# Cross-attention and a ternary feed-forward on one core: another lead-in, and the exponential taken while the transposed banks are read

## The chip, the cores and the metric

One NeuronCore of a Trainium2 chip. TensorE, VectorE, ScalarE, GpSimd and SyncE each run one instruction stream in order; they meet through semaphores. The metric is the device time of one execution in microseconds. Three runs of the kernel before took 98.30, 98.36 and 98.38 us, median 98.36.

## The reference, cut to what matters

```python
x = x + xattn(layernorm(x), ctx_512, Wq, Wkv_expand, Wout)
x = x + ffn(layernorm(x), w_gate, w_up, w_down)

def xattn(q, latent_kv, Wq, Wkv_expand, Wout):   # q (16, 56, 256), latent_kv (16, 1500, 64)
    kv = latent_kv @ Wkv_expand.T                # Wkv_expand (512, 64): 256 rows for k, 256 for v
    # 16 heads of 16; causal mask from query 0 and key 0
    attn = softmax(where(causal, qh @ kh.T / 4, min))
    return (attn @ vh) @ Wout.T

def ffn(x, w_gate, w_up, w_down):                # 256 -> 1024 -> 256
    # each weight: scale = mean(|w|), values -1, 0, 1; each token: scale = max(|x|) / 127, rounded
    return qlinear(silu(qlinear(x, w_gate)) * qlinear(x, w_up), w_down)
```

There are 56 queries, so the causal mask leaves the first 56 of the 1500 keys of each batch; only these are loaded.

## The kernel before, in words

The 16 batches of 56 tokens are 896 tokens, 7 tiles of 128. Attention goes by 8 pairs of batches (u = 0 to 7). All of it is float32 but the ternary feed-forward products. The order of the work is written out by hand: a lead-in, called slot -1, then slots 0 to 17. Each engine runs through the same slots and takes from each the work that tables at the top of the file give it (lines 22 to 68). In slot s TensorE does the scores of pair s, the transposes of the attention of pair s - 2, the transposes of the probabilities of pair s - 1, the jobs that `MISC_JOBS` lists for the slot (line 41), an output projection where `OP_SLOTS` has one, and the products of pair s - 1 with v (lines 1130 to 1149). From slot 8 on it does gate and up products, transposes of the rounded hidden values, and the down products.

Every small product goes into one of four PSUM banks, taken in turn: job number n writes bank n mod 4 when the job n - 4 has been read (`take_bank`, line 904). `VECTOR_READS` (line 49) says which of these banks VectorE reads; ScalarE reads the others (`read_misc`, line 336).

**The lead-in.** SyncE issues the loads x0, ctx0, ctx1, x1, x2 and the weights of the feed-forward; ScalarE's queue issues wkv, wq, ctx2, ctx3 (lines 34 and 35). The four ctx loads move rows of 256 bytes (one key of one batch) to 56 partitions each, the wkv load rows of 256 bytes too. When wkv has landed, ScalarE writes it out twice side by side (line 323), so that four 128x128 transposes (line 939) give `wkvT` with the same 64 rows on both halves of the partitions. TensorE meanwhile runs nine products of zeros (`warm_up`, line 1076), then the jobs wkvT, three more products of zeros, ctxT (line 945: waits for all four ctx loads), two more, wqT, the first quarter of k of batches 0 to 7, xT of tile 0, and q of pair 0. The first two tiles' layer norm is done by VectorE with GpSimd's reciprocal root (lines 471 and 683), tiles 2 to 6 by GpSimd (`first_layer_norm`, line 463: two small operations, a power, one normalising operation).

**k.** `kT` holds k transposed; `k_wide` holds it once for each of four heads with the other heads' rows zeroed (`widen`, line 286), so that one product gives the scores of four heads. The first part is widened by VectorE and GpSimd in the lead-in, the rest by GpSimd in slots 0 to 3. Index c of `kT` is the half of the batches (0 to 7, 8 to 15); c = 1 is computed in slot 2.

**Softmax.** VectorE takes the maxima out of PSUM (line 715) and writes the differences into `probs` (line 724). ScalarE exponentiates them in place (line 567). TensorE transposes them, eight 128x128 transposes into two banks (line 1031). ScalarE copies the banks into `pT` (job kind "tr", line 367). TensorE multiplies with v; VectorE divides by the sums (line 730).

**The slots around it.** `ABS_SLOTS` puts the sum of magnitudes of the three weights to slot 1 (VectorE), 2 and 3 (ScalarE); a product with a constant matrix (job kind "mean") gives the scale, ScalarE reads it, and VectorE inverts it in the same slot (`invert_weight_scale`, line 798), ahead of the next slot's division of the attention. ScalarE loads the tables for silu behind its other work of slot 7 (line 570).

Of the kernel before, what the change touches and what calls it, by code (L numbers as in the profile page):

```python
# [24 lines left out]
LN1_SLOTS = {-1: [2], 0: [3], 1: [4], 2: [5], 3: [6]}  # L25
# [26 lines left out]

EXP_BEHIND = {0: 3}
# [17 lines left out]
def xattn_ffn(nc, x, ctx_512, wq, wkv, wout, w_gate, w_up, w_down, out):  # L71
# [38 lines left out]
    DV = 2  # L110
# [30 lines left out]
    with ExitStack() as ctx:  # L141
# [28 lines left out]
        probs = sb("probs", [P, R, NH, Q])  # L170
# [48 lines left out]
        ctx2_in = sem("ctx2_in")  # L219
        wkv_in, wq_in, wo_in, wkv_ready = sem("wkv_in"), sem("wq_in"), sem("wo_in"), sem("wkv_ready")  # L220
# [20 lines left out]
        exp_ready, rden_ready = sem("exp_ready"), sem("rden_ready")  # L241
# [44 lines left out]
        def widen(eng, ops, slot, engine):  # L286
            for c, hf, g in WIDENINGS.get((slot, engine), []):
                j0, j1 = KEY_GROUPS[c][g]
                cols = slice(2 * S * j0, 2 * S * j1)
                n = 2 * S * (j1 - j0)  # L290
                const(eng, "head_mask")
                wait_read(eng, *[job for job in K_JOBS if job[1] == c and job[2][0] <= j0 < job[2][1] and hf in job[3]])
                ops.tensor_tensor(k_wide[:, c, hf, :, cols], kT[:, c, hf, None, cols].to_broadcast([P, RH, n]),  # L293
                                  head_mask[:, 0:RH, None].to_broadcast([P, RH, n]),
                                  ALU.mult).then_inc(kw_ready[c][g], 1)
# [15 lines left out]
        def load(eng, name):  # L311
# [91 lines left out]
        def _(pool):  # L403
# [141 lines left out]
        def _(act):  # L545
# [17 lines left out]
            def exponentials(s):  # L563
                u = s
                if 0 <= u < NP:
                    act.wait_ge(sub_ready, u + 1)
                    nc.scalar.activation(probs[:, u % R, :, 0:S], probs[:, u % R, :, 0:S],  # L567
                                         ACT.Exp).then_inc(exp_ready, 1)

            def load_silu_tables(s):  # L570
                if s == NP - 1:
                    load_tables(ACT.Silu)
# [55 lines left out]
            for s in range(NT_SLOT0):  # L628
                read_attention(s - 2)
                read_probabilities(s)  # L630
                read_misc_banks(s, 0, EXP_BEHIND.get(s, 0))
                exponentials(s)
                read_misc_banks(s, EXP_BEHIND.get(s, 0), None)
                ternary_signs(s)
                sum_magnitudes(s)
                load_silu_tables(s)
            for s in range(NT_SLOT0, SLOTS):
                if s == NT_SLOT0:
                    read_attention(s - 2)
                read_probabilities(s)  # L640
# [9 lines left out]
        def _(dve):  # L650
# [18 lines left out]
            nc.vector.memset(probs[:, :, :, S:], 0.0).then_inc(pads_ready, 1)  # L669
# [25 lines left out]
            widen(dve, nc.vector, -1, "vector")  # L695
# [22 lines left out]
            def subtract_maxima(s):  # L718
                u = s
                if u < NP:  # L720
# [3 lines left out]
                    nc.vector.tensor_tensor(probs[:, u % R, :, 0:S].rearrange("p (r h) k -> p r h k", r=2),  # L724
# [134 lines left out]
            for s in range(NT_SLOT0):  # L859
# [15 lines left out]
                widen_k(s)  # L875
# [24 lines left out]
        def _(pe):  # L900
# [9 lines left out]
            def write_values(i):  # L910
# [3 lines left out]
                wait_read(pe, ("wkvT", 0), ("ctxT", 0))  # L914
# [13 lines left out]
            def write_misc(job):  # L928
# [245 lines left out]
```

## Time and profile before

| | us |
|---|---|
| median of 3 runs (98.30 to 98.38) | 98.36 |
| span of the profiled execution | 99.1 |
| TensorE busy (share of the span) | 81.9 (83%) |
| VectorE busy | 72.4 (73%) |
| ScalarE busy | 58.6 (59%) |
| GpSimd busy | 56.9 (57%) |

The profile is of one execution, whose span is 99.1 us; its starts are counted from the first instruction. In the rows PE is TensorE, PEld its weight loads, DVE VectorE, ACT ScalarE, POOL GpSimd. A float32 product shows as two passes ("x8" for four products), a transpose as one. Many products are recorded by one helper (line 902), so they are told apart by their tiles: `sc` is the scores' PSUM, `bank` one of the four banks, `sc<-tern` the products of zeros. The starts of the first score products of a slot (`sc<-causal,sel`) mark the slots.

### The profile page before, as it was taken

What the parts mean: (1) busy time and instruction counts of PE and PEld (TensorE: products, weight loads), DVE (VectorE), ACT (ScalarE), POOL (GpSimd) and SP (SyncE); (2) the same over time, 40 slices, a digit from 0 to 9 for tenths busy, and PEclk for the clock granted to TensorE, in tenths of its full rate; (3) what the DMA queues carried; (4) which work ended last, traced back from release to release, by engine and by line L of the source; (5) the groups of instructions that cost most, each with busy time, mean ns of one, the idle gap of its engine ahead of it and who ended that gap; (6) DMA issues with size and microseconds to landing.
All of it is one profiled execution on the core that took longest, in us unless ns stands there. A gap on an engine that the chain in (4) does not pass through costs nothing.

```text
span 99.1 us, 2411 instructions
## 1 busy us (share of the span) xinstructions
PE 81.9 (83%) x872; PEld 57.4 (58%) x872; DVE 72.4 (73%) x180; ACT 58.6 (59%) x98; POOL 56.9 (57%) x109
## 2 busy tenths in 40 slices
PE   4964968976989985999999998699938589998680
PEld 1323645744865874878696876585514256665460
DVE  4650243978995898189976999637899999999741
ACT  0730241363528794657979699964565496988520
POOL 5640064739930989879693982526165651786650
PEclk9997599999999999999999999999999999999999
DMA  2999998000000000000089451800000000011123
GB/s 35 286 285 353 350 362 320 13 0 0 0 0 7 0 3 3 7 0 0 0 60 161 99 119 25 187 0 0 0 7 0 0 0 0 3 53 53 60 82 130
DMA packets 12579, 7.59 MB, mean 77 GB/s; under 512 B 7960, under 2 KB 12312, under 8 KB 12568
## 3 DMA queue, kind: packets, MB, share of 16 engines
q1 hardware_dynamic: 11292, 6.93, 26.1%
q10 hardware_dynamic: 1276, 0.51, 2.0%
q8 instruction: 7, 0.11, 0.5%
q14 instruction: 4, 0.03, 0.1%
HBM read 4.95 MB, written 0.92 MB: 59 GB/s over the span
## 4 chain that ended last, share of the span: by engine, by line
DVE 41%; PE 37%; issue 7%; DMA 6%; POOL 2%; ACTq 2%; ACT 1%; POOLq 0%; DVEq 0%
PE bank L902 21%; DVE amax L820 9%; DVE h_sb L813 7%; PE sc L902 7%; DMA ctx_sb<-in_ctx_dram 6%; DVE probs L724 4%; PE bank L1031 4%; DVE v_wide L655 3%; PE bank L1055 2%; DVE asum L708 2%; DVE mx L715 2%; DVE xnT L656 2%; DVE attn L739 2%; DVE s_tok L827 1%; DVE x_sb L755 1%
## 5 line engine op out<-in xcount | busy, mean ns | idle before, releaser
L293 POOL TENSOR_TENSOR k_wide<-kT,head_mask 128x896 f32<-128x896 f32 (+1 forms) x9 | 13.2, 1481 | 12.0 <-ACT kT L557 12.0
L902 PE MATMUL sc<-wT,xqT 128*128 128x512 bf16 x56 | 13.9, 380 | 3.4 <-DVE h_sb L813 3.4
L306 POOL TENSOR_SCALAR wf_sb<-h_sb,r_tok 128x512 f32<-128x512 f32 x13 | 9.1, 714 | 10.5 <-DVE r_tok L834 10.5
L612 ACT ACTIVATE wf_sb<-sc,s_out 128x512 f32<-128x512 f32 x14 | 9.6, 689 | 7.5 <-PE sc L902 5.1
L715 DVE TENSOR_REDUCE mx<-sc 128x16 f32<-128x896 f32 x8 | 8.7, 1090 | 3.6 <-PE sc L902 3.4
L813 DVE SCALAR_TENSOR_TENSOR h_sb<-sc,s_out,wf_sb 128x512 f32<-128x512 f32 x14 | 9.9, 740 | 1.1 <-ACT wf_sb L612 1.1
L902 PEld LDWEIGHTS sc<-wT,xqT 128*128 128x128 bf16 x56 | 5.0, 98 | 9.2 <-DVE h_sb L813 5.1
L567 ACT ACTIVATE probs<-probs 128x896 f32<-128x896 f32 x8 | 7.6, 952 | 4.2 <-DVE probs L724 3.8
L902 PEld LDWEIGHTS bank<-v_wide,pT 128*64 128x64 f32 x256 | 8.1, 138 | 2.3 <-issue 2.3
L902 PE MATMUL bank<-xnT,wqT 128*128 128x224 f32 (+1 forms) x40 | 7.4, 329 | 2.1 <-DVE xnT L656 1.5
L902 PE MATMUL bank<-v_wide,pT 128*64 128x34 f32 x256 | 9.0, 225 | 0.0
L724 DVE TENSOR_TENSOR probs<-sc,mx 128x896 f32<-128x896 f32 x8 | 8.7, 1084 | 0.1
L820 DVE TENSOR_REDUCE amax<-h_sb 128x1 f32<-128x1024 f32 x7 | 8.5, 1220 | 0.2
L557 ACT ACTIVATE pT<-bank 128x448 f32<-128x448 f32 x16 | 7.8, 542 | 1.4 <-PE bank L1031 1.0
L1031 PE MATMUL bank<-ident,probs 128*128 128x128 f32 x64 | 8.4, 273 | 0.0
L557 ACT ACTIVATE hT<-bank 128x1024 bf16<-128x1024 f16 (+1 forms) x7 | 6.7, 962 | 2.2 <-PE bank L1112 1.4
L902 PE MATMUL bank<-woT,attnT 128*128 128x256 f32 x28 | 7.6, 394 | 0.4 <-ACT attnT L557 0.4
L902 PEld LDWEIGHTS bank<-xnT,wqT 128*128 128x128 f32 x40 | 6.2, 190 | 2.9 <-issue 2.9
L902 PE MATMUL sc<-k_wide,qT 64*64 64x224 f32 x128 | 7.4, 349 | 0.0
L1031 PEld LDWEIGHTS bank<-ident,probs 128*128 128x128 f32 x64 | 7.2, 141 | 0.3 <-ACT probs L567 0.3
L902 PE MATMUL bank<-wdT,hT 128*128 128x256 bf16 x56 | 7.1, 273 | 0.0
L902 PE MATMUL sc<-tern 128*128 128x512 bf16 x14 | 5.9, 577 | 1.3 <-DVE tern L659 1.3
(108 smaller groups left out, 167.9 us busy)
## 6 DMA issues: line engine op xcount, KB each, us to landing
wf_sb<-in_L_ffn_w_gate_dram SPq DMA_DIRECT2D x1, 1024.0 KB, 9.0
wf_sb<-in_L_ffn_w_up_dram SPq DMA_DIRECT2D x1, 1024.0 KB, 11.1
wf_sb<-in_L_ffn_w_down_dram SPq DMA_DIRECT2D x1, 1024.0 KB, 12.6
out_dram<-k_wide SPq DMA_DIRECT2D x7, 128.0 KB, 1.7
x_sb<-in_x_dram SPq DMA_DIRECT2D x2, 256.0 KB, 4.4
x_sb<-in_x_dram SPq DMA_DIRECT2D x1, 384.0 KB, 6.5
wq_sb<-in_L_xattn_Wq_dram ACTq DMA_DIRECT2D x1, 256.0 KB, 4.5
wo_sb<-in_L_xattn_Wout_dram SPq DMA_DIRECT2D x1, 256.0 KB, 9.2
```

The lines of the kernel that those rows point to most:

```text
L293: ops.tensor_tensor(k_wide[:, c, hf, :, cols], kT[:, c, hf, None, cols].to_broadcast([P, RH, n]), head_mask[:, 0:RH, None].to_broadcast([P ...
L306: ops.tensor_scalar(h_int[:, t % 2, c, :], h_sb[:, t % 3, GC * c:GC * c + GC], r_tok[:, 1, t:t + 1], CODED, ALU.mult, ALU.add).then_inc(hi ...
L557: return nc.scalar.activation(dst, src, ACT.Copy, scale=scale, bias=bias)
L567: nc.scalar.activation(probs[:, u % R, :, 0:S], probs[:, u % R, :, 0:S], ACT.Exp).then_inc(exp_ready, 1)
L612: nc.scalar.activation(g_sb[:, t % 2, GC * c:GC * c + GC], SC[:, j % 4, :], ACT.Silu, scale=s_out[:, 0, t:t + 1]).then_inc(silu_ready, 1)
L655: return nc.vector.tensor_scalar(dst, src, scale, 1.0, ALU.mult, ALU.mult)
L715: nc.vector.tensor_reduce(mx[:, u % R, :].rearrange("p (r h) -> p r h", r=2), scores_of(u), axis=AX_X, op=ALU.max).then_inc(max_ready, 1)
L724: nc.vector.tensor_tensor(probs[:, u % R, :, 0:S].rearrange("p (r h) k -> p r h k", r=2), scores_of(u), mx[:, u % R, :].rearrange("p (r h) ...
L813: nc.vector.scalar_tensor_tensor(h_sb[:, t % 3, cols], SC[:, j % 4, :], s_out[:, 1, t:t + 1], g_sb[:, t % 2, cols], ALU.mult, ALU.mult).th ...
L820: nc.vector.tensor_reduce(amax[:, 1, t:t + 1], h_sb[:, t % 3, :], axis=AX_X, op=ALU.max, apply_absolute_value=True).then_inc(h_amax_ready, 1)
L902: return nc.tensor.matmul(*a, **k)
L1031: last = nc.tensor.transpose(bank[:, P * m:P * m + P], probs[:, u % R, h0:h0 + 2, :].rearrange("p h k -> p (h k)"), ident[:, :])
```

## The change

It does seven things.

1. ctx is loaded with rows of 512 bytes (two keys that follow one another) to 28 partitions by each of the four loads; wkv with rows of 1024 bytes. On ScalarE's queue the order becomes wkv, ctx2, ctx3, wq. x is loaded in parts of 1, 2 and 4 tiles.
2. ScalarE no longer writes wkv twice. The transposes of wkv and ctx become plain products with the identity, each done twice, to the upper and to the lower 64 partitions of a bank. wkvT is two jobs, one bank read by ScalarE and one by VectorE, and ctxT is two, the second at the end of the lead-in; the readers put the columns in order with a stride.
3. The first part of k is widened out of PSUM by VectorE for both halves; `kT` and GpSimd are left out for it.
4. GpSimd's layer norm in the lead-in takes tiles 1 and 2, VectorE's only tile 0. All of the other widenings for c = 0 are GpSimd's in slot 0, ahead of the layer norm of tile 3.
5. The k products for c = 1 move from slot 2 to slot 0, between those for c = 0; in slot 0, q of pair 1 comes before v.
6. The differences (`shifted`, with a large negative number in the padding) are transposed, and ScalarE exponentiates while it reads the transposed banks. The separate exponential goes. The tables for silu are loaded behind the last of these, in slot 8.
7. `VECTOR_READS` keeps only parts of wkvT, ctxT and k; the banks of v, xT and woT go to ScalarE.

```diff
-LN1_SLOTS = {-1: [2], 0: [3], 1: [4], 2: [5], 3: [6]}
+LN1_SLOTS = {-1: [1, 2], 0: [3], 1: [4], 2: [5], 3: [6]}
...
-WARM_MORE = {('wkvT', 0): 3, ('ctxT', 0): 2}
-X_PARTS = [(0, 2), (2, 4), (4, 7)]
+WARM_MORE = {('wkvT', 1): 3, ('ctxT', 0): 1}
+X_PARTS = [(0, 1), (1, 3), (3, 7)]
...
-ACT_LOADS = ['wkv0', 'wq0', 'ctx2', 'ctx3', 'tables', 'twice']
+ACT_LOADS = ['wkv0', 'ctx2', 'ctx3', 'wq0', 'tables']
...
-MISC_JOBS = {-1: [('wkvT', 0), ('ctxT', 0), ('wqT', 0), ('k', 0, K_FIRST, (0, 1)), ('xT', 0), ('q', 0, 1)],
-             0: [('k', 0, K_REST, (0,)), ('k', 0, K_REST, (1,)), ('xT', 1), ('v', 0), ('v', 2), ('q', 1, 2)],
+MISC_JOBS = {-1: [('wkvT', 0), ('wkvT', 1), ('ctxT', 0), ('wqT', 0), ('k', 0, K_FIRST, (0, 1)), ('xT', 0), ('q', 0, 1), ('ctxT', 1)],
+             0: [('k', 0, K_REST, (0,)), ('k', 1, K_ALL, (0,)), ('k', 0, K_REST, (1,)), ('k', 1, K_ALL, (1,)),
+                 ('xT', 1), ('q', 1, 2), ('v', 0), ('v', 2)],
              1: [('xT', 2), ('xT', 3), ('q', 2, 4)],
-             2: [('k', 1, K_ALL, (0,)), ('k', 1, K_ALL, (1,)), ('v', 1), ('v', 3)],
+             2: [('v', 1), ('v', 3)],
...
-VECTOR_READS = [('ctxT', 0), ('xT', 1), ('xT', 2), ('xT', 3), ('xT', 4), ('xT', 5), ('xT', 6), ('k', 0, K_REST, (1,)),
-                ('k', 1, K_ALL, (1,)), ('v', 0), ('v', 1), ('woT', 0)]
+VECTOR_READS = [('wkvT', 1), ('ctxT', 0), ('k', 0, K_FIRST, (0, 1)), ('k', 0, K_REST, (1,))]
...
-KEY_GROUPS = [[(0, 1), (1, 2), (2, 4)], [(0, 2), (2, 4)]]
-WIDENINGS = {(-1, 'vector'): [(0, 0, 0)],
-             (-1, 'gpsimd'): [(0, 1, 0)],
-             (0, 'gpsimd'): [(0, 0, 1), (0, 1, 1)],
-             (1, 'gpsimd'): [(0, 0, 2), (0, 1, 2)],
-             (2, 'gpsimd'): [(1, 0, 0), (1, 1, 0)],
-             (3, 'gpsimd'): [(1, 0, 1), (1, 1, 1)]}
+KEY_GROUPS = [[(1, 2), (2, 4)], [(0, 2), (2, 4)]]
+WIDENINGS = {0: [(0, 0, 0), (0, 1, 0), (0, 0, 1), (0, 1, 1)],
+             2: [(1, 0, 0), (1, 1, 0)],
+             3: [(1, 0, 1), (1, 1, 1)]}
...
-    DV = 2
+    DV = 1
...
             elif kind == "ctx":
...
-                eng.dma_start(ctx_sb[S * par:S * par + S, :, c, :],
-                              ctx_512[b0:2 * PJ * (c + 1):2, 0:S, :].rearrange("b k l -> k b l")).then_inc((ctx_in, ctx2_in)[c], 16)
-            elif kind == "twice":
-                eng.wait_ge(wkv_in, 16)
-                nc.scalar.activation(wkv_sb[:, :, :, :], wkv_in_sb[:, :, None, :].to_broadcast([P, 4, 2, L]),
-                                     ACT.Copy).then_inc(wkv_ready, 1)
+                eng.dma_start(ctx_sb[S // 2 * i:S // 2 * i + S // 2, :, :],
+                              ctx_512[i::4, 0:S, :].rearrange("b (k e) l -> k b (e l)", e=2)).then_inc(ctx_in, 16)
...
             if kind == "wkvT":
-                last = copy(wkvT[:, :], bank[:, :])
+                last = copy(wkvT[:, :].rearrange("l (p o) -> l o p", o=4)[:, 2 * i:2 * i + 2, :],
+                            bank[:, 0:2 * P].rearrange("l (o p) -> l o p", o=2))
...
+            elif kind == "k" and job[2] == K_FIRST:
+                const(eng, "head_mask")
+                for hf in job[3]:
+                    last = nc.vector.tensor_tensor(k_wide[:, i, hf, :, 0:2 * S],
+                                                   bank[:, None, 2 * S * hf:2 * S * hf + 2 * S].to_broadcast([P, RH, 2 * S]),
+                                                   head_mask[:, 0:RH, None].to_broadcast([P, RH, 2 * S]), ALU.mult)
...
-                last = copy(pT[:, i % 2, n0:n0 + 4 * 2 * S].rearrange("p (m b q) -> p m b q", m=4, b=2),
-                            bank[:, :].rearrange("p (m b q) -> p m b q", m=4, b=2)[:, :, :, 0:S])
+                last = nc.scalar.activation(pT[:, i % 2, n0:n0 + 4 * 2 * S].rearrange("p (m b q) -> p m b q", m=4, b=2),
+                                            bank[:, :].rearrange("p (m b q) -> p m b q", m=4, b=2)[:, :, :, 0:S], ACT.Exp)
...
-                    pe.wait_ge(wkv_ready, 1)
-                    for o in range(4):
-                        last = nc.tensor.transpose(bank[:, P * o:P * o + P],
-                                                   wkv_sb[:, o, :, :].rearrange("p e l -> p (e l)"), ident[:, :])
+                    pe.wait_ge(wkv_in, 16)
+                    for o in range(2):
+                        for c in range(2):
+                            last = mm(bank[Q * c:Q * c + Q, P * o:P * o + P], wkv_sb[:, 2 * i + o, :], ident[:, :],
+                                      start=True, stop=True)
...
-                pe.wait_ge(ctx_in, 32)
-                pe.wait_ge(ctx2_in, 32)
-                for j in range(PJ):
-                    last = nc.tensor.transpose(bank[:, 2 * S * j:2 * S * j + 2 * S], ctx_sb[:, j, :, :].rearrange("p c l -> p (c l)"),
-                                               ident[0:2 * S, 0:2 * S])
+                    pe.wait_ge(ctx_in, 64)
+                    for e in range(2):
+                        for c in range(2):
+                            last = mm(bank[Q * c:Q * c + Q, 2 * S * e:2 * S * e + 2 * S],
+                                      ctx_sb[:, 2 * c + i, L * e:L * e + L], ident[0:2 * S, 0:2 * S], start=True, stop=True)
...
+                if u == 0:
+                    wait_read(pe, ("k", 0, K_FIRST, (0, 1)))
...
-                pe.wait_ge(exp_ready, u + 1)
+                pe.wait_ge(sub_ready, u + 1)
```

## Rows read from the trace of the kernel before

**Rows 1.** The page: TensorE's clock in 40 slices; the chain by engine

```profile
PEclk9997599999999999999999999999999999999999
...
DVE 41%; PE 37%; issue 7%; DMA 6%; POOL 2%; ACTq 2%; ACT 1%; POOLq 0%; DVEq 0%
```

**Rows 2.** The chain of waits in order of time: start, length (us), what

```profile
2.61 6.11 DMA ctx_sb<-in_ctx_dram
```

**Rows 3.** Timeline of TensorE, lead-in: start, length (us), line, operation, [idle before it, releaser]

```profile
1.27 4.02 PE L902 MATMUL sc<-tern 128*128 128x512 bf16 x9 [1.27 <-DVE tern L659]
5.40 0.63 PE L939 MATMUL bank<-ident,wkv_sb 128*128 128x128 f32 x4
...
8.86 0.98 PE L945 MATMUL bank<-ident,ctx_sb 112*128 112x112 f32 x4 [2.18 <-DMA ctx_sb<-in_ctx_dram]
...
10.49 1.06 PE L960 MATMUL bank<-ident,wq_sb 128*128 128x128 f32 x4
...
13.39 1.12 PE L902 MATMUL bank<-xnT,wqT 128*128 128x112 f32 x8 [0.52 <-issue]
15.16 0.38 PE L902 MATMUL sc<-causal,sel 64*64 64x448 bf16 x4 [0.65 <-ACT qT L557]
```

**Rows 4.** Timeline of TensorE, slots 0 to 2

```profile
17.92 1.10 PE L902 MATMUL bank<-wkvT,ctxT 64*64 64x128 f32 x32
...
20.70 0.38 PE L902 MATMUL sc<-causal,sel 64*64 64x448 bf16 x4 [0.60 <-ACT qT L557]
...
23.30 0.41 PE L968 MATMUL bank<-ident,xn_sb 128*128 128x128 f32 x2 [0.22 <-POOL xn_sb L460]
...
27.05 0.38 PE L902 MATMUL sc<-causal,sel 64*64 64x448 bf16 x4
...
29.87 1.77 PE L902 MATMUL bank<-ctxT,wkvT 64*128 64x448 f32 x4
```

**Rows 5.** Timeline of the other engines, end of the lead-in

```profile
13.00 0.62 DVE L293 TENSOR_TENSOR k_wide<-kT,head_mask 128x448 f32<-128x448 f32 x1 [2.50 <-ACT kT L557]
13.04 1.38 POOL L293 TENSOR_TENSOR k_wide<-kT,head_mask 128x448 f32<-128x448 f32 x1 [6.60 <-ACT kT L557]
...
14.54 0.36 ACT L557 ACTIVATE qT<-bank 128x224 f32<-128x224 f32 x1 [1.25 <-PE bank L902]
```

**Rows 6.** Timeline of GpSimd, slot 0

```profile
21.45 0.19 POOL L447 TENSOR_SCALAR veps<-mv 128x1 f32<-128x1 f32 x1 [1.94 <-DVE mv L677]
...
22.61 0.55 POOL L460 TENSOR_SCALAR xn_sb<-x_sb,negm,rstd 128x256 f32<-128x256 f32 x1 [0.19 <-POOL rstd L454]
```

**Rows 7.** Instruction groups kept apart by shape: count, busy us, mean ns, idle before

```profile
L293 POOL TENSOR_TENSOR k_wide<-kT,head_mask 128x896 f32<-128x896 f32 x6 | 10.0, 1680 | 4.0 <-ACT kT L557 4.0
...
L557 ACT ACTIVATE pT<-bank 128x448 f32<-128x448 f32 x16 | 7.8, 542 | 1.4 <-PE bank L1031 1.0
L567 ACT ACTIVATE probs<-probs 128x896 f32<-128x896 f32 x8 | 7.6, 952 | 4.2 <-DVE probs L724 3.8
...
L592 ACT ACTIVATE tern<-wf_sb 128x2048 bf16<-128x2048 f32 x2 | 3.8, 1916 | 0.0
...
L557 ACT ACTIVATE v_wide<-bank,parity_mask 128x512 f32<-128x512 f32 x4 | 2.6, 703 | 2.3 <-PE bank L902 2.3
L547 ACT ACT_TABLE_LOAD x2 | 2.6, 1283 | 3.1 <-issue 3.1
```

**Rows 8.** Timeline of TensorE, slots 3 to 8

```profile
38.81 1.75 PE L902 MATMUL bank<-xnT,wqT 128*128 128x224 f32 x8 [0.93 <-DVE xnT L656]
...
41.58 1.13 PE L902 MATMUL bank<-v_wide,pT 128*64 128x34 f32 x32
42.64 0.38 PE L902 MATMUL sc<-causal,sel 64*64 64x448 bf16 x4
...
67.27 1.04 PE L902 MATMUL sc<-wT,xqT 128*128 128x512 bf16 x4
```

**Rows 9.** Timeline of ScalarE, slot 8

```profile
67.97 0.69 ACT L612 ACTIVATE wf_sb<-sc,s_out 128x512 f32<-128x512 f32 x1 [1.87 <-PE sc L902]
```

More of the change, by code:

```diff
@@ L148, in xattn_ffn @@
         x_sb = sb("x_sb", [P, NT, C])
-        ctx_sb = sb("ctx_sb", [2 * S, PJ, 2, L])
+        ctx_sb = sb("ctx_sb", [2 * S, 2 * 2, 2 * L])
         wq_sb = sb("wq_sb", [P, HALVES, C])
-        wkv_in_sb = sb("wkv_in_sb", [P, 4, L])
-        wkv_sb = sb("wkv_sb", [P, 4, 2, L])
+        wkv_sb = sb("wkv_sb", [P, 4, L])
         wo_sb = sb("wo_sb", [P, HALVES, C])
@@ L284, in x_part, with widen @@
             return next(i for i, (a, b) in enumerate(X_PARTS) if a <= t < b)
[L286 to L295, printed above, removed]
+        def widen(eng, ops, c, hf, g):
+            j0, j1 = KEY_GROUPS[c][g]
+            cols = slice(2 * S * j0, 2 * S * j1)
+            n = 2 * S * (j1 - j0)
+            const(eng, "head_mask")
+            wait_read(eng, *[job for job in K_JOBS if job[1] == c and job[2][0] <= j0 < job[2][1] and hf in job[3]])
+            ops.tensor_tensor(k_wide[:, c, hf, :, cols], kT[:, c, hf, None, cols].to_broadcast([P, RH, n]),
+                              head_mask[:, 0:RH, None].to_broadcast([P, RH, n]),
+                              ALU.mult).then_inc(kw_ready[c][g], 1)
         x_v = x.rearrange("b s c -> (b s) c").rearrange("(t p) c -> p t c", p=P)
@@ L341, in read_misc @@
             if kind == "wkvT":
-                last = copy(wkvT[:, :], bank[:, :])
+                last = copy(wkvT[:, :].rearrange("l (p o) -> l o p", o=4)[:, 2 * i:2 * i + 2, :],
+                            bank[:, 0:2 * P].rearrange("l (o p) -> l o p", o=2))
             elif kind == "ctxT":
-                last = copy(ctxT[:, 0:KT], bank[:, 0:KT])
+                last = copy(ctxT[:, KT // 2 * i:KT // 2 * i + KT // 2].rearrange("l (k e) -> l e k", e=2),
+                            bank[:, 0:KT // 2].rearrange("l (e k) -> l e k", e=2))
+            elif kind == "k" and job[2] == K_FIRST:
+                const(eng, "head_mask")
+                for hf in job[3]:
+                    last = nc.vector.tensor_tensor(k_wide[:, i, hf, :, 0:2 * S],
+                                                   bank[:, None, 2 * S * hf:2 * S * hf + 2 * S].to_broadcast([P, RH, 2 * S]),
+                                                   head_mask[:, 0:RH, None].to_broadcast([P, RH, 2 * S]), ALU.mult)
             elif kind == "k":
@@ L474, in _ @@
                                         ALU.pow).then_inc(rstd_first, 1)
-            widen(pool, nc.gpsimd, -1, "gpsimd")
             first_layer_norm(-1)
             def widen_k(s):
-                widen(pool, nc.gpsimd, s, "gpsimd")
+                for c, hf, g in WIDENINGS.get(s, []):
+                    widen(pool, nc.gpsimd, c, hf, g)
             def second_variance(s):
@@ L561, in _ @@
                     read_misc(act, copy, job)
[L563 to L572, printed above, removed]
             def read_misc_banks(s, first, last):
@@ L581, in read_attention, with exponentials @@
                     read_misc(act, copy, ("aT", u))
-            def read_probabilities(s):
+            def exponentials(s):
                 u = s - 1
@@ L587, in read_probabilities @@
                     read_misc(act, copy, ("tr", u, 1))
+                if u == NP - 1:
+                    load_tables(ACT.Silu)
             def sum_magnitudes(s):
@@ L639, in _ @@
                     read_attention(s - 2)
-                read_probabilities(s)
+                exponentials(s)
                 read_misc_banks(s, 0, None)
@@ L874, in _ @@
                 invert_weight_scale(s)
-                widen_k(s)
             for s in range(NT_SLOT0, SLOTS):
@@ L913, in write_values @@
                 assert misc_no[jobs[1]] == misc_no[jobs[0]] + 1
-                wait_read(pe, ("wkvT", 0), ("ctxT", 0))
+                wait_read(pe, ("wkvT", 0), ("wkvT", 1), ("ctxT", 0), ("ctxT", 1))
                 pe.wait_ge(pads_ready, 1)
@@ L950, in write_misc @@
                     n = 2 * S * (j1 - j0)
-                    wait_read(pe, ("wkvT", 0), ("ctxT", 0))
+                    wait_read(pe, ("wkvT", 0), ("wkvT", 1), ("ctxT", 0), *[("ctxT", 1)] * (j1 > 2))
                     for k, hf in enumerate(hfs):
@@ L1132, in _ @@
                 transpose_attention(s - 2)
-                transpose_probabilities(s)
+                transpose_scores(s)
                 misc_products(s)
@@ L1139, in _ @@
                     transpose_attention(s - 2)
-                transpose_probabilities(s)
+                transpose_scores(s)
                 misc_products(s)
```

28 lines of the change are left out of this document (9 added, 19 removed).

## The prediction

> **What bounds the kernel now.** I read the page first: the clock by slices and the chain by engine [rows 1]. The chain is shared by VectorE (41%) and TensorE (37%): TensorE carries the attention slots, VectorE the feed-forward at the end, which the change doesn't touch. Transfers hold 6%, all of it one wait [rows 2]: the last ctx load, issued at 2.61, lands 6.11 later, at 8.7. The timeline of TensorE [rows 3] shows what that does: it idles 2.18 us before ctxT, and from there to about 12.4 the granted clock falls from 1.0 to 0.5, which is 1.2 of 2.4 GHz (slices of 2.48 us [rows 1]). The same four transposes take 0.63 at 5.40 and 1.06 at 10.49. So the lead-in waits for ctx and then pays the half clock; the first scores start at 15.16. I follow the starts of the scores, S0 to S4, and of the first gate product.
>
> **The lead-in.** wkvT starts at 5.40, when the nine products of zeros end [rows 3]; those stay, so an earlier wkv gains nothing. ctx: on ScalarE's queue 240 KB now stand up to the end of the last ctx load, instead of 496 KB with wq. By bytes, 6.11 becomes 2.96, and it lands by 5.6 (an estimate; upper end the old 6.11, landing at 8.7). It is needed at about 7.3, so the idle stretch goes and the clock stays up. wq, moved behind ctx, has the place that ctx had; landing at 8.7 at worst, it would cost 1 us.
>
> From 5.40 TensorE has: wkvT, 8 products or 16 passes of 128 columns on 64 output partitions. No row shows such a pair of tiles with many columns. v runs 32 passes of 128 columns on four tiles at once in 1.10 [rows 4], 0.034 a pass; on two tiles I take 0.069, so 1.10 (other end: one after the other, 0.137 a pass, 2.2). Four products of zeros: the first nine took 4.02/9 = 0.45 each; I take half, by the ratio of the transposes at the two clocks, so 0.9 (other end 1.8). The first ctxT job, 8 passes of 112 columns: 0.48 (other end 0.96). wqT 0.63. First k, 4 passes: half of q's 1.12, 0.56. xT 0.31. The sum ends at 9.4. ScalarE copies xT (0.4, from 0.36 for 224 columns [rows 5]), q takes 1.12, its copy 0.36, and the scores follow 0.26 later as now: **S0 = 11.5** instead of 15.16, 3.65 earlier. The second ctxT job (0.48) lies beside q's copy and costs nothing; without that cover it costs 0.48. VectorE widens k out of PSUM at 0.62 a half [rows 5], from 9.1 to 10.3: before S0, and in place of a copy and GpSimd's 1.38. Strided reads of the halves: nothing (0.2 at most), since the products of zeros lie behind them.
>
> **Slot 0.** It took 5.54 (to 20.70 [rows 4]). It gets the k passes of c = 1, 1.77 in slot 2 now. They use the other 64 rows than those of c = 0 between them, so between none and all of it is added; I take half, 0.9. q before v removes the wait of 0.60 for q's copy but adds one of some 0.4 for ScalarE's copy of xT, behind the k copies. S1 = 11.5 + 6.25 = 17.75.
>
> **Slot 1: GpSimd.** The gain meets GpSimd here. VectorE's moments of tile 1 come behind its widening, about 10.9. A layer norm takes 1.71 (21.45 to 23.16 [rows 6]); two end at 14.3. Then all four widenings of c = 0 stand ahead of tile 3's norm: two of 1.68 [rows 7] and two half as wide at 0.9, to 19.5, and the norm to 21.2. xT of tile 3 is at 21.35, where it was at 23.30 [rows 4]: only 1.95 earlier, TensorE waiting over 1 us for it. ScalarE is as late: both v reads (2.6 [rows 7], half of it VectorE's now) start at 17.8, and the two reads with the exponential (0.54 each) end at 21.4. From xT to S2 it was 3.75; copied 0.25 sooner, 3.5: **S2 = 24.85**, 2.2 earlier.
>
> **Slots 2 and 3: ScalarE.** Slot 2 loses the 1.77. But both v reads are ScalarE's again, and behind them stands the read of the mean, for which VectorE waits before it divides the attention of pair 1, for which TensorE waits. The wait that TensorE has for VectorE's copies now (0.93 ahead of 38.81 [rows 8]) goes over to ScalarE with them. v is written at S2 + 3.3 (scores, transposes and v, some 1.1 each as v's row), read at + 5.9, and the transposed attention comes at about + 7. ScalarE's sum of magnitudes (2.1 with its end [rows 7]) runs to + 8.1; then come that attention, two exponentials, woT and two xT: 0.4 + 1.0 + 0.6 + 0.8, to + 10.9. Only then can q of pairs 4 and 5 start; from there to S4 it is 3.83 (38.81 to 42.64 [rows 8]). **S4 = 24.85 + 14.8 = 39.65**, 3.0 earlier.
>
> **The exponential.** Eight instructions of 0.95 leave ScalarE [rows 7]; the reads of the banks stay at 16 and I price them the same (0.54; upper end, the rate of 0.95 for twice the columns, is no dearer). Between the difference and the transposes a stage of 1 us goes, but a slot later TensorE has long other work, so this gains little: 0.2 in slots 4 to 7, where it is busy throughout (0 to 0.6). The silu tables (1.28 [rows 7], 1.5 with the dummy) move into slot 8, where ScalarE idles 1.87 before the first silu [rows 9]: nothing; without that cover up to 1.5. The gate product, at 67.27 [rows 8], so comes 3.2 earlier, and the rest follows unchanged. The profiled execution spans 99.1, 0.7 above the median of 98.36; a gain of 3.2 gives about 95.9 of span and **95.2 of time**.
>
> **The rivals.**
>
> *A serial lead-in:* if the paired passes don't overlap, S0 and all behind it come 1.6 later: 96.8. For it: no row shows two tiles of 128 rows with many columns at once. Against it: four tiles do overlap.
>
> *GpSimd dearer:* a widening beside VectorE's took 1.38 instead of 0.9 [rows 5]. If all four in slot 0 are slowed by half, S2 comes 2.6 later: 97.8. Against it: the wide ones all took 1.68, with VectorE busy or not.
>
> *ctx no earlier:* if the rows' length and place don't matter, ctxT starts near 8.7, at the half clock again: 1.4 of wait and some 1.4 of clock, 98.0. The change would then not do what it says.
>
> *Slower: weight loads in the open.* The place is the 24 passes of wkvT and ctxT: if each pair waits for its weight load, a pass costs 0.137 and as much again for the load, 6.6 instead of 1.6, and the time is 100.2. It decides from 3.2 us on, that is, when a pass costs more than 0.2. Against it: the products with v, on the same tiles, do 32 passes with 32 loads in 1.13 [rows 8], 0.035 each.
>
> The Trainium skill (TensorE: Matmul & The Clock Gate, section Part 3: Packing small matmuls, "What overlaps and what doesn't") lets a weight load overlap running products only when the row group differs; these pairs share all rows, so by it the last rival would hold, 100.2 against 95.2. The trace disagrees in the row just named.
>
> *More gain:* if GpSimd and ScalarE delay TensorE less than I place it, up to 3.65 + 0.6 stays: 94.1.
>
> **How the numbers follow.** Forecast 0.62 (its own range 94.3 to 96.2: the k passes overlapping wholly or not at all, 0.9 either way, much of it absorbed by GpSimd, and the products of zeros at their other end, 0.9 up); serial 0.12; GpSimd 0.08; ctx no earlier 0.06; slower 0.05; more gain 0.07. The range takes in the forecast, the serial case and half of more gain: 94.0 to 97.1. What a measurement can tell from no change is about 0.2% (0.2 us). Faster 0.92 (all but the slower case and half of "ctx no earlier"), same 0.03, slower 0.05.
>
> **What would show it.** Right: no wait of TensorE for ctx, the clock whole in slices 4 and 5, S0 at 11 to 12; GpSimd busy without a break up to xT of tile 3, and TensorE waiting for it; in slots 2 and 3 waits for attention and xT behind ScalarE; the gate product at 63 to 65. Wrong: wkvT's 16 passes lasting over 2 us, or VectorE's dividing or the maxima ending TensorE's waits in slots 1 to 3, or a gap before the first silu over 0.3 us longer than TensorE's products need.

## The result, and the profile after

Over 20 executions each, the median is 98.98 us (97.05 to 100.91) for the changed kernel and 98.44 (98.01 to 104.95) for the kernel before; the ratio of comparable executions is 0.9905, 95% interval [0.9875, 0.9934]. Median and ratio point opposite ways because the ratio leaves out the slow executions, 15 of the changed kernel's 20. Its executions differ by the granted clock: 4 of the 20 have a mean of 1.0 and took 97.05 to 97.71, the other 16 have 0.966 to 0.983 and took 98.22 to 100.91. So the change is worth about 1% where the clock stays whole; where it falls, that is lost again, with some 0.5 us on top. 95.2 was forecast, 94.0 to 97.1.

The profiled execution is one with a fallen clock: span 97.5, time 99.23, mean clock 0.982. Its page, clock by slices and chain (cf. [rows 1]):

```profile
PEclk9999999997599999999999999999999999999999
...
PE 39%; DVE 25%; POOL 10%; issue 8%; ACT 7%; DMA 6%; ACTq 1%; POOLq 0%; DVEq 0%
```

The dip has moved from slices 4 and 5 to slices 10 and 11, which is 21.9 to 26.8 us (slices of 2.44), and GpSimd has gone from 2% of the chain to 10%. The timeline of TensorE (start, length, line, operation, [idle before it, releaser]), to be read beside [rows 3, 4, 8]:

```profile
5.22 1.41 PE L881 MATMUL bank<-ident,wkv_sb 128*64 128x128 f32 x16
...
8.47 0.65 PE L940 MATMUL bank<-ident,wq_sb 128*128 128x128 f32 x4 [0.23 <-DMA wq_sb<-in_L_xattn_Wq_dram]
...
10.64 1.12 PE L881 MATMUL bank<-xnT,wqT 128*128 128x112 f32 x8 [0.52 <-issue]
...
12.40 0.38 PE L881 MATMUL sc<-causal,sel 64*64 64x448 bf16 x4
...
13.47 1.77 PE L881 MATMUL bank<-ctxT,wkvT 64*128 64x336 f32 x8
...
18.17 0.37 PE L881 MATMUL sc<-causal,sel 64*64 64x448 bf16 x4
...
22.20 0.41 PE L948 MATMUL bank<-ident,xn_sb 128*128 128x128 f32 x2 [1.66 <-POOL xn_sb L455]
23.18 3.33 PE L881 MATMUL bank<-xnT,wqT 128*128 128x224 f32 x8 [0.56 <-ACT xnT L552]
...
27.49 0.38 PE L881 MATMUL sc<-causal,sel 64*64 64x448 bf16 x4
...
34.41 0.41 PE L1037 MATMUL bank<-ident,attn 128*128 128x128 f32 x2 [1.07 <-DVE attn L722]
...
37.76 1.75 PE L881 MATMUL bank<-xnT,wqT 128*128 128x224 f32 x8 [1.18 <-ACT xnT L552]
...
41.58 0.38 PE L881 MATMUL sc<-causal,sel 64*64 64x448 bf16 x4
...
65.69 1.04 PE L881 MATMUL sc<-wT,xqT 128*128 128x512 bf16 x4
```

Two things are to be seen. The lead-in did what was forecast: no wait for ctx, transposes of wq at 0.65 instead of 1.06, S0 at 12.40 instead of 15.16. And in slot 1 TensorE waits 1.66 for GpSimd, does 0.41 of work, waits 0.56 for ScalarE, and then needs 3.33 for the eight passes of q that take 1.75 at 37.76. The stretches of 20 to 23 and 23 to 26 us (stretch and length, then busy time with number of instructions of TensorE, its weight loads, VectorE, ScalarE and GpSimd, then granted clock, share and GB/s of the transfers) show what came with it:

```profile
20.00:23.00 3.00, 0.95 (x7) 0.50 (x5) 2.93 (x5) 2.34 (x6) 2.42 (x8) 1.00 0.00 0
23.00:26.00 3.00, 2.83 (x8) 2.52 (x8) 1.30 (x1) 0.03 (x1) 2.79 (x4) 0.50 0.01 3
```

TensorE works 0.95 of the 3 us before, and behind them the granted clock is 0.50, 1.2 of 2.4 GHz. That the one causes the other is tried below. The timeline of GpSimd shows what it waited for:

```profile
15.16 5.10 POOL L287 TENSOR_TENSOR k_wide<-kT,head_mask 128x448 f32<-128x448 f32 x4
...
21.50 0.56 POOL L455 TENSOR_SCALAR xn_sb<-x_sb,negm,rstd 128x256 f32<-128x256 f32 x1 [0.18 <-POOL rstd L449]
```

The four widenings stand ahead of the layer norm of tile 3, as forecast, and at the forecast price (two of 1.68 and two of 0.9 are 5.16).

### The profile page after: what moved, and what is told of

Read it like the earlier page. It is cut to its first block, busy times and chain, and to the rows that moved or that the text cites. A ratio compares the mean times of both kernels' runs of the same rounds, so it can differ in the third digit from the quotient of the medians.

```text
span 97.5 us, 2460 instructions
## 1 busy us (share of the span) xinstructions
PE 81.4 (84%) x895; PEld 58.1 (60%) x895; DVE 66.8 (68%) x168; ACT 56.3 (58%) x101; POOL 56.4 (58%) x111
## 4 chain that ended last, share of the span: by engine, by line
PE 39%; DVE 25%; POOL 10%; issue 8%; ACT 7%; DMA 6%; ACTq 1%; POOLq 0%; DVEq 0%
PE bank L881 22%; DVE amax L800 9%; PE sc L881 7%; DVE h_sb L793 7%; DMA wq_sb<-in_L_xattn_Wq_dram 6%; PE bank L1013 5%; POOL k_wide L287 5%; PE bank L1037 3%; ACT v_wide L552 2%; ACT tern L579 2%; POOL rstd L449 2%; POOL xn_sb L455 1%; DVE k_wide L338 1%; DVE s_tok L807 1%; DVE shifted L707 1%
## 5 line engine op out<-in xcount | busy, mean ns | idle before, releaser
L442 POOL TENSOR_SCALAR veps<-mv 128x1 f32<-128x1 f32 x13 | 2.5, 192 | 17.4 <-DVE mv L661 11.3
L287 POOL TENSOR_TENSOR k_wide<-kT,head_mask 128x896 f32<-128x896 f32 (+1 forms) x8 | 11.7, 1494 | 0.0
L881 PE MATMUL bank<-xnT,wqT 128*128 128x224 f32 (+1 forms) x40 | 9.0, 375 | 2.9 <-ACT xnT L552 1.7
L881 PEld LDWEIGHTS bank<-xnT,wqT 128*128 128x128 f32 x40 | 7.3, 218 | 3.9 <-issue 3.7
L707 DVE TENSOR_TENSOR shifted<-sc,mx 128x896 f32<-128x896 f32 x8 | 8.7, 1085 | 0.1
L1013 PE MATMUL bank<-ident,shifted 128*128 128x128 f32 x64 | 8.4, 274 | 0.0
L552 ACT ACTIVATE attnT<-bank 128x224 f32<-128x224 f32 x8 | 2.9, 361 | 8.1 <-PE bank L1037 8.1
L552 ACT ACTIVATE qT<-bank 128x448 f32<-128x448 f32 (+1 forms) x5 | 2.3, 470 | 9.0 <-PE bank L881 9.0
L1013 PEld LDWEIGHTS bank<-ident,shifted 128*128 128x128 f32 x64 | 7.2, 141 | 0.3 <-issue 0.3
## 6 DMA issues: line engine op xcount, KB each, us to landing
wf_sb<-in_L_ffn_w_up_dram SPq DMA_DIRECT2D x1, 1024.0 KB, 11.5
```

Source lines behind the costliest of these rows:

```text
L552: return nc.scalar.activation(dst, src, ACT.Copy, scale=scale, bias=bias)
L707: nc.vector.tensor_tensor(shifted[:, u % R, :, 0:S].rearrange("p (r h) k -> p r h k", r=2), scores_of(u), mx[:, u % R, :].rearrange("p (r ...
L881: return nc.tensor.matmul(*a, **k)
L1013: last = nc.tensor.transpose(bank[:, P * m:P * m + P], shifted[:, u % R, h0:h0 + 2, :].rearrange("p h k -> p (h k)"), ident[:, :])
```

## The experiments

Two theories stood against each other, and each turned out to hold a part. The first (A): the execution profiled before was not a usual one, since its lead-in ran at the half clock [rows 1, 3], so a good part of the gain was never to be had. The rival: the gain is there, and slot 1 takes it back, through the wait for GpSimd or through the clock behind it.

**The kernel before, unchanged, profiled again.**

> The kernel before, unchanged, looked at once more. Theory A: the execution profiled before (span 99.1) was longer than its usual one, because the granted clock fell to half from 8.7 to 12.4 us; usually the wait for ctx in the lead-in costs only the idle time. Then this profile shows a whole clock in slices 4 and 5, a span of 96.4 to 97.0, and the first scores at 12.6 to 13.2 instead of 15.16. Rival: the clock falls there in every execution; the span is 98.5 to 99.2 and the first scores start near 15.2. Time 98.3 to 98.6 by both.

Median 98.51, ratio 1.0025 [0.9993, 1.0058]. The profiled execution has span 97.0 and time 98.69, and its clock is whole in all 40 slices. Its timeline of TensorE:

```profile
8.33 0.57 PE L945 MATMUL bank<-ident,ctx_sb 112*128 112x112 f32 x4 [1.53 <-DMA ctx_sb<-in_ctx_dram]
...
13.06 0.38 PE L902 MATMUL sc<-causal,sel 64*64 64x448 bf16 x4 [0.65 <-ACT qT L557]
...
24.95 0.38 PE L902 MATMUL sc<-causal,sel 64*64 64x448 bf16 x4
...
65.18 1.04 PE L902 MATMUL sc<-wT,xqT 128*128 128x512 bf16 x4
```

A holds. S0 is at 13.06, where [rows 3] have 15.16, and the gate product at 65.18, where [rows 8] have 67.27: 2.1 us of both belong to that one execution. Of these, 0.53 is ctxT starting later (8.86 against 8.33) and 1.57 the half clock (from ctxT to S0 6.30 against 4.73). There is a second thing in it. Time less span is 98.69 − 97.0 = 1.7 here and 99.23 − 97.5 = 1.7 for the changed kernel, so the span of 99.1 stood for a time of 100.8 and not for one near the median.

**The changed kernel with tile 3's norm between the narrow and the wide widenings.** Same work, other order on GpSimd.

```diff
             for s in range(NT_SLOT0):
-                widen_k(s)
+                widen_k(s, 0, 2)
                 first_layer_norm(s)
+                widen_k(s, 2, None)
```

> The changed kernel with GpSimd's layer norm of tile 3 put between the two narrow and the two wide widenings of slot 0. Theory B (GpSimd's order makes TensorE idle 1.66 us in slot 1, and the clock then falls and costs another 1.6): tile 3 is normalised by 18.8 instead of 22.06, TensorE then waits only for ScalarE's reads of v (until 20.95) and of xT, about 1.4 us in all instead of 2.2; the third scores start at 24.6 to 25.2 with the clock whole, time 96.2 to 96.8; at 97.5 to 98.5 where the clock still falls. Rival (ScalarE alone sets the slot): the third scores stay within 0.3 us of where they are with a whole clock, 25.9, time 97.0 to 97.3.

Median 96.84, ratio 0.9823 [0.9772, 0.9873], clock whole. TensorE:

```profile
18.26 0.37 PE L882 MATMUL sc<-causal,sel 64*64 64x448 bf16 x4
...
21.00 0.44 PE L949 MATMUL bank<-ident,xn_sb 128*128 128x128 f32 x2 [0.37 <-ACT v_wide L553]
22.50 1.75 PE L882 MATMUL bank<-xnT,wqT 128*128 128x224 f32 x8 [1.06 <-ACT xnT L553]
...
25.24 0.38 PE L882 MATMUL sc<-causal,sel 64*64 64x448 bf16 x4
...
32.16 0.41 PE L1038 MATMUL bank<-ident,attn 128*128 128x128 f32 x2 [1.07 <-DVE attn L723]
...
63.42 1.04 PE L882 MATMUL sc<-wT,xqT 128*128 128x512 bf16 x4
```

xT of tile 3 comes 1.20 earlier. From S1 to S2 it is 6.98 instead of 9.32: of these 2.34, 1.58 are q at the whole clock (1.75 against 3.33), and the rest is the shorter wait, which ScalarE, at v's reads and the exponentials, now ends. S2 at 25.24 and the median of 96.84 lie just over the upper ends expected, 25.2 and 96.8. The gate product is 2.27 earlier. So GpSimd's order costs 2.3 where the clock falls.

**The changed kernel with TensorE kept at work during that wait.** Five products of zeros into the bank that xT of tile 3 overwrites; GpSimd is as late as before.

```diff
                 elif kind == "xT":
+                    if i == 3:
+                        for _ in range(5):
+                            mm(bank[:, :], warm[:, 0:P], warm[:, :], start=True, stop=True)
```

> The changed kernel with five products of zeros on TensorE, written to the bank of xT of tile 3 ahead of its wait for GpSimd, so that the wait stays and the idle time goes. Theory B: the clock stays whole in slot 1, q of pairs 2 and 3 takes 1.75 instead of 3.33, the third scores start near 25.9 instead of 27.49, and the time is 97.0 to 97.4, 1.6 to 1.9 under the changed kernel's median of 98.98. Rival (the 3.33 us come from something else than the idle time ahead, such as GpSimd or the reads): q stays at 3.3, time 98.8 to 99.3.

Median 97.19, ratio 0.9879 [0.983, 0.9929]; mean granted clock 0.998. TensorE:

```profile
18.02 0.37 PE L881 MATMUL sc<-causal,sel 64*64 64x448 bf16 x4
...
20.77 1.25 PE L881 MATMUL bank<-tern 128*128 128x512 bf16 x5 [0.37 <-ACT v_wide L552]
21.94 0.44 PE L951 MATMUL bank<-ident,xn_sb 128*128 128x128 f32 x2
22.94 1.75 PE L881 MATMUL bank<-xnT,wqT 128*128 128x224 f32 x8 [0.56 <-ACT xnT L552]
...
25.68 0.38 PE L881 MATMUL sc<-causal,sel 64*64 64x448 bf16 x4
```

This parts the wait from the clock. Tile 3 waits for GpSimd as long as in the changed kernel (3.92 from S1 to its transposes, 4.03 there), but q takes 1.75 and S1 to S2 is 7.66: against 9.32 the clock costs 1.66, and against 6.98 the wait alone 0.68. Products that compute nothing bring the median to where the changed kernel's executions with the whole clock are (97.05 to 97.71). None of the six executions here has a granted clock under 0.998. Of the changed kernel's 32 (20 above and 12 below) 23 are under 0.99. So the idle time is the cause of the fall, and the fall that of the 3.33.

**The kernel before with the exponential alone.** The reads of the transposed banks do the exponential, the separate one goes, the silu tables move to slot 8.

```diff
-                last = copy(pT[:, i % 2, n0:n0 + 4 * 2 * S].rearrange("p (m b q) -> p m b q", m=4, b=2),
-                            bank[:, :].rearrange("p (m b q) -> p m b q", m=4, b=2)[:, :, :, 0:S])
+                last = nc.scalar.activation(pT[:, i % 2, n0:n0 + 4 * 2 * S].rearrange("p (m b q) -> p m b q", m=4, b=2),
+                                            bank[:, :].rearrange("p (m b q) -> p m b q", m=4, b=2)[:, :, :, 0:S], ACT.Exp)
...
-                    nc.scalar.activation(probs[:, u % R, :, 0:S], probs[:, u % R, :, 0:S],
-                                         ACT.Exp).then_inc(exp_ready, 1)
...
+                if u == NP - 1:
+                    load_tables(ACT.Silu)
...
-            nc.vector.memset(probs[:, :, :, S:], 0.0).then_inc(pads_ready, 1)
+            nc.vector.memset(probs[:, :, :, S:], NEG).then_inc(pads_ready, 1)
...
-                pe.wait_ge(exp_ready, u + 1)
+                pe.wait_ge(sub_ready, u + 1)
```

> The kernel before with the exponential alone moved into the reads of the transposed banks, and the silu tables into slot 8; lead-in, slots and readers as before. My theory: little, since TensorE has other work in between: 0.2 to 0.6 us less than before, time 97.8 to 98.3. Rival (the stage of 1 us per pair is on the path in the early slots): 1 to 2 us less, 96.4 to 97.4. Other rival (the tables land on the path in slot 8): 0.5 to 1.5 us more.

Median 98.15, ratio 0.9976 [0.9935, 1.0017]: no difference that these runs can tell. S0 and the gate product on TensorE:

```profile
12.56 0.38 PE L901 MATMUL sc<-causal,sel 64*64 64x448 bf16 x4 [0.65 <-ACT qT L557]
...
64.36 1.04 PE L901 MATMUL sc<-wT,xqT 128*128 128x512 bf16 x4
```

They are 51.80 apart; in the kernel before, profiled again, 52.12. That is 0.3, against 0.2 forecast, and all of it lies between the last scores and the gate product (9.07 from S7 on, 9.39 in the kernel before, profiled again). ScalarE's busy time falls to 52.1 from 58.6, and almost none of it was on the path.

**The kernel before with the order of ScalarE's queue alone.** ctx keeps its short rows and wkv its copy.

```diff
-ACT_LOADS = ['wkv0', 'wq0', 'ctx2', 'ctx3', 'tables', 'twice']
+ACT_LOADS = ['wkv0', 'ctx2', 'ctx3', 'wq0', 'tables', 'twice']
```

> The kernel before with one line changed: on ScalarE's queue wq goes behind ctx2 and ctx3, rows as short as before. Theory C (the order, not the row length or the rest of the lead-in, removes the wait for ctx, and wq is late in its place): ctx lands by 6.5, TensorE no longer waits for it, but waits for wq, which lands at 8.2 to 8.8; the first scores start 0.2 to 0.7 earlier than in the kernel before with a whole clock (13.06), time 97.8 to 98.3. Rival (rows of 256 bytes are what makes ctx late): ctx still ends TensorE's wait, after 7.5, and the time stays at 98.3 to 98.6.

Median 98.29, ratio 0.997 [0.9938, 1.0001]. TensorE's lead-in:

```profile
7.24 0.55 PE L945 MATMUL bank<-ident,ctx_sb 112*128 112x112 f32 x4
...
8.18 0.66 PE L960 MATMUL bank<-ident,wq_sb 128*128 128x128 f32 x4
...
12.11 0.38 PE L902 MATMUL sc<-causal,sel 64*64 64x448 bf16 x4 [0.65 <-ACT qT L557]
```

One moved word takes the wait for ctx away, and S0 is as early as in the changed kernel (12.40, and 12.02 in the repeat below). With the old order it was 13.06 and, in the run with the exponential alone, 12.56; so the gain at S0 is 0.45 to 0.95, which the medians don't tell from none. wq is late in its place: it lands at 8.2, and S0 follows 3.93 behind the start of its transposes. In the changed kernel it is the same to 0.01 (8.47 to 12.40; 8.08 to 12.02 in the repeat). So longer rows, plain products for transposes and k widened out of PSUM added nothing to S0 that can be seen; what they would bring with wq earlier, no run here parts.

**The changed kernel, norm first, with some reads given back to VectorE.** ScalarE was late in slots 1 to 3.

```diff
-VECTOR_READS = [('wkvT', 1), ('ctxT', 0), ('k', 0, K_FIRST, (0, 1)), ('k', 0, K_REST, (1,))]
+VECTOR_READS = [('wkvT', 1), ('ctxT', 0), ('k', 0, K_FIRST, (0, 1)), ('k', 0, K_REST, (1,)),
+                ('xT', 2), ('xT', 3), ('v', 0), ('v', 1)]
...
-SUB_BEHIND = {0: 2, 1: 2}
+SUB_BEHIND = {0: 1, 1: 2}
...
-                read_misc_banks(s, SUB_BEHIND.get(s, 0), None)
                 first_moments(s)
+                read_misc_banks(s, SUB_BEHIND.get(s, 0), None)
```

> The kernel with tile 3's norm ahead of the wide widenings, and the reads of half of v and of xT of tiles 2 and 3 given back to VectorE. Theory D (what is left of the waits in slots 1 to 3 is ScalarE's queue): the wait of 1.06 before q of pairs 2 and 3 shrinks to 0.3 or less and that of 1.07 before the attention of pair 1 by 0.5 or more; the third scores come at 24.1 to 24.6 instead of 25.24, the fifth at 37.5 to 38.6 instead of 39.33, time 95.3 to 96.2. Rival (VectorE becomes late in ScalarE's place): time 96.6 to 97.2.

Median 95.19, ratio 0.9687 [0.9658, 0.9716]. TensorE:

```profile
5.01 1.09 PE L883 MATMUL bank<-ident,wkv_sb 128*64 128x128 f32 x16
...
7.81 0.66 PE L942 MATMUL bank<-ident,wq_sb 128*128 128x128 f32 x4
...
11.74 0.38 PE L883 MATMUL sc<-causal,sel 64*64 64x448 bf16 x4
...
20.94 1.75 PE L883 MATMUL bank<-xnT,wqT 128*128 128x224 f32 x8 [0.85 <-DVE xnT L642]
...
25.28 0.41 PE L1039 MATMUL bank<-ident,attn 128*128 128x128 f32 x2 [0.46 <-DVE attn L724]
...
30.04 0.41 PE L1039 MATMUL bank<-ident,attn 128*128 128x128 f32 x2
...
33.38 1.75 PE L883 MATMUL bank<-xnT,wqT 128*128 128x224 f32 x8 [1.18 <-ACT xnT L554]
...
37.21 0.38 PE L883 MATMUL sc<-causal,sel 64*64 64x448 bf16 x4
```

S4 is at 37.21, 2.12 earlier than with the norm first alone. But 0.75 of that is no work of this edit: S0 is at 11.74 here and at 12.49 there, and wkvT, the same instructions, took 1.09 here and 1.96 there. From S0 to S4 it is 25.47 instead of 26.84, so the shared reads are worth 1.37. With the norm first alone TensorE waited 1.07 (32.16) for the attention of pair 1; at 30.04 there is none, and 0.46 stand before that of pair 0 instead. The wait for q of pairs 2 and 3 was to shrink to next to nothing and did not: 0.85, now for VectorE. The 1.18 ahead of q of pairs 4 and 5 stands as it did, behind ScalarE's sum of magnitudes.

**The changed kernel, unchanged, profiled again.**

> The changed kernel, unchanged, looked at once more. Theory B: TensorE idles over 2 us in slot 1 in every execution, and the clock falls behind it in most of them: most times 98.8 to 99.3, the others 97.0 to 97.8; a profile with a whole clock would have q of pairs 2 and 3 at 1.75, the third scores at 25.7 to 26.1 and a span of 95.3 to 96.0. Rival (the first measurement of it was disturbed): most times at 97.0 to 97.8.

Median 98.46, ratio 0.989 [0.9861, 0.9918]; 7 of 12 executions have a mean granted clock of 0.966 to 0.983. The profiled one is one of them, and its TensorE shows the same figure:

```profile
21.79 0.41 PE L948 MATMUL bank<-ident,xn_sb 128*128 128x128 f32 x2 [1.64 <-POOL xn_sb L455]
22.76 3.33 PE L881 MATMUL bank<-xnT,wqT 128*128 128x224 f32 x8 [0.57 <-ACT xnT L552]
```

The fall is a trait of the kernel and no accident of one execution. Both profiled executions of this kernel are ones in which it came, so no trace shows it with the whole clock.

**A version that beats both.** The kernel with shared reads, with wq on SyncE's queue and x's second part on ScalarE's, and with one product of zeros behind wkvT in place of three and one.

```diff
-WARM_MORE = {('wkvT', 1): 3, ('ctxT', 0): 1}
+WARM_MORE = {('wkvT', 1): 1}
...
-SYNC_LOADS = ['x0', 'ctx0', 'ctx1', 'x1', 'x2', 'f0', 'wo0', 'f1', 'f2']
-ACT_LOADS = ['wkv0', 'ctx2', 'ctx3', 'wq0', 'tables']
+SYNC_LOADS = ['x0', 'ctx0', 'ctx1', 'wq0', 'x2', 'f0', 'wo0', 'f1', 'f2']
+ACT_LOADS = ['wkv0', 'ctx2', 'ctx3', 'x1', 'tables']
```

> The last but one kernel (shared reads) with wq on SyncE's queue ahead of x, tiles 1 and 2 of x on ScalarE's behind ctx, and one product of zeros instead of four between the lead-in's transposes. Theory C (the lead-in now waits for wq and for its products of zeros): wqT starts by 7.9 instead of 8.6, the first scores at 11.4 to 11.9, time 0.5 to 0.9 under the kernel with shared reads. Rival (VectorE's widening of k or GpSimd's norms set the start of slot 1 anyway): within 0.2 of it. Other rival (fewer products let the clock fall in the lead-in): 1 to 2 us more.

Median 94.78 (94.09 to 94.96), ratio 0.9638 [0.9611, 0.9665], clock whole. TensorE:

```profile
7.03 0.66 PE L942 MATMUL bank<-ident,wq_sb 128*128 128x128 f32 x4 [0.29 <-DMA wq_sb<-in_L_xattn_Wq_dram]
...
10.96 0.38 PE L883 MATMUL sc<-causal,sel 64*64 64x448 bf16 x4
```

wq's transposes start 0.78 earlier than in the run with shared reads (7.81 there) and S0 follows by the same 0.78 (11.74 there). In both it is wq's landing that they start at, 7.0 here and 7.8 there. That wkvT starts at 4.70 instead of 5.01, the first products of zeros having ended sooner, adds nothing to it: TensorE still waits 0.29 for wq. The median gains 0.41, less than the 0.5 to 0.9 expected; the profiled execution, at 94.09, is the fastest of the six.

## Why the prediction was wrong

| event | forecast | changed kernel | same, norm first |
|---|---|---|---|
| S0 | 11.5 | 12.40 | 12.49 |
| S1 | 17.75 | 18.17 | 18.26 |
| xT of tile 3 | 21.35 | 22.20 | 21.00 |
| S2 | 24.85 | 27.49 | 25.24 |
| S4 | 39.65 | 41.58 | 39.33 |
| first gate product | 64.1 | 65.69 | 63.42 |

**The step that failed is the baseline:** "The profiled execution spans 99.1, 0.7 above the median of 98.36; a gain of 3.2 gives about 95.9 of span and 95.2 of time". It set a span against times. By the 1.7 between the two, that execution took 100.8, 2.4 above the median, and the text itself had named the cause, the half clock behind the wait for ctx. Of the 3.65 forecast at S0, 2.10 was no gain over a usual execution of the kernel before: 1.57 the half clock, 0.53 a ctx that landed later. The span of 95.9 came out, since the changed kernel's executions with the whole clock have 95.3 to 96.0; but in part this is luck, as errors cancel on the way. Less the 1.58 that q lost to the clock, S2 is 1.06 later than forecast, S4 0.35 later, and the gate product on time. With 1.7 added it would have been 97.6, against 97.05 to 97.71 measured.

**The second step is one left out.** "TensorE waiting over 1 us for it" was right (1.66), and the same text had shown the clock at half behind a wait of 2.18 [rows 3]. The forecast gave the new wait no such price. It costs 3.33 − 1.75 = 1.6 in most executions (16 of 20), which takes the 97.3 of those with the whole clock to 98.9; the median is 98.98. That the wait is what brings the clock down was shown by filling it: with the products of zeros q takes 1.75.

The other steps:

- *ctx earlier, clock whole in the lead-in:* right, but the order of the queue alone is enough for it. wq is late next, as the upper end had it: it lands 6.13 after its issue, at 8.4, and TensorE waits 0.23.
- *S0:* the mechanism was right, the terms mis-sized by 0.9 together. wkvT took 1.41 (1.10 priced), ctxT 0.60 (0.48), k 0.69 (0.56), xT 0.44 (0.31). wq stood in the sum with nothing, and its transposes, at 7.9 by the sum, began at 8.47, when it had landed. The chain of the profiled execution begins with it (start, length, what; cf. [rows 2]):

```profile
2.29 6.13 DMA wq_sb<-in_L_xattn_Wq_dram
```

  In the run with shared reads wkvT took 1.09, the price taken, wq landed at 7.8, and S0 was at 11.74, 0.2 late.
- *Slot 0:* 5.77 against 6.25. The k passes of both halves of the batches take 1.77 together, and those of c = 0 took 1.39 in the kernel before, profiled again; so c = 1 adds 0.38 and not 0.9: they overlap for the most part.
- *GpSimd in slot 0:* right in order and price.
- *Slots 2 and 3:* S2 to S4 took 14.09 against 14.8; the waits stand where they were placed, 1.07 for VectorE's attention and 1.18 for xT behind ScalarE.
- *The exponential:* 0.3 against 0.2 forecast. The reads of the banks kept their price of [rows 7] with the exponential in them (groups by shape: count, busy time, mean ns):

```profile
L367 ACT ACTIVATE pT<-bank 128x448 f32<-128x448 f32 x16 | 7.9, 551 | 0.5
```

- *The silu tables:* they cost nothing, as forecast. ScalarE has loaded them before the first gate product is done (timeline of ScalarE):

```profile
64.27 1.28 ACT L542 ACT_TABLE_LOAD   x1
...
66.39 0.69 ACT L599 ACTIVATE wf_sb<-sc,s_out 128x512 f32<-128x512 f32 x1 [0.35 <-PE sc L881]
```

Of the rivals, *serial lead-in* and *weight loads in the open* are excluded by the run with shared reads, whose 16 passes of wkvT take 1.09 together with their 16 loads (timeline of the weight loads):

```profile
5.01 0.85 PEld L883 LDWEIGHTS bank<-ident,wkv_sb 128*64 128x64 f32 x16 [0.63 <-POOL ident_h L404]
```

The Trainium skill (TensorE: Matmul & The Clock Gate, section Part 3: Packing small matmuls, "What overlaps and what doesn't") lets a load overlap only when the row group differs; these pairs share all 128 rows, and the row of wkvT's passes disagrees: one after the other they would have taken 2.2, by the prediction's 0.137 a pass. *ctx no earlier* and *GpSimd dearer* are excluded by their rows above, and *more gain* did not come: TensorE waited for GpSimd and ScalarE where it was placed.

What stays open: why the clock falls in some executions of the same kernel and not in others. In the lead-in of the kernel before, a wait of 2.18 went with a fall and one of 1.53 without, as did one of 1.25 in the run with the exponential alone. The kernel before has falls of its own: 6 of 23 executions run beside the first experiments and 4 of 23 beside the last have a mean granted clock of 0.918 to 0.983 and took 100.6 to 106.4. Where in the kernel those come, no profile shows but the one of [rows 1]. No kernel was made to vary the length of the wait alone.

## What to carry to other kernels

Before a gain is worked out from one profiled execution, set its time, not its span, beside the median, and if its clock shows a dip, ask what of the gain is only that dip's recovery. A wait of TensorE that is forecast wants a second price, what its passes cost behind it at the half clock; here that was 1.6 us, more than the 0.7 that the wait itself added. Here, reordering one engine's work, so that what TensorE needs comes before what is needed a slot later, or a few products of zeros in the wait, kept the clock at 0.998 or more in all twelve executions of the two runs.

## What was not expected of the hardware

- Writing a copy out of PSUM with a stride costs time from some stride on. wkvT's read writes every fourth value (16 bytes apart): 0.63 on ScalarE and 0.61 on VectorE for 256 columns, where copies of xT, 256 side by side, take 0.41 in the mean on ScalarE and 0.42 on VectorE (in the kernel before). ctxT's read writes every second value (8 bytes): 0.39 for 224 columns on VectorE and 0.37 on ScalarE, whose copies of q, 224 side by side, take 0.36: next to nothing more. The timeline of VectorE:

```profile
6.68 0.61 DVE L640 COPY wkvT<-bank 128x256 f32<-128x256 f32 x1 [0.89 <-PE bank L881]
7.96 0.39 DVE L640 COPY ctxT<-bank 128x224 f32<-128x224 f32 x1 [0.67 <-PE bank L881]
```

  The Trainium skill (SBUF — State Buffer, section "Door 1: The DMA port swizzle", the note on SBUF cachelines) says that accesses to one 16-byte line go at full rate when two or more fall into it. These rows agree: two values to a line cost next to nothing, one value to a line costs 0.2. The note goes on to give 4 fp32 values as a stride that is still free; at that stride the rows of wkvT disagree.
- The first products run at little more than half their later rate although the granted clock is shown as 1.00: nine of zeros take 4.02 from 1.27 on (0.45 each), five take 1.25 at 20.77 (0.25 each). wkvT's passes stand where the one rate gives way to the other, and the same 16 passes took 1.09 to 1.96 in the six profiles that have them. The longest, 1.96, is 0.12 a pass, and the shortest 0.07, so I take it that the change came behind them in the one and ahead of them in the other. The prediction halved the price of the later products of zeros by the two granted clocks; they did take about half, but the first nine stand at a granted clock of 1.00. What decides when the change comes wasn't tried.
